# L1 attention: TensorE's small products in a new order over the two images of a pair

## The chip, the cores and the metric

The kernel runs on one core of one Trainium2 chip. The metric is the device time of one execution in microseconds (us). The kernel before takes 2540.39 us, the median of 3 runs (2538.69 to 2540.77).

## What is computed

Two layers of a small vision tower over 128 images of 64 tokens with 64 features: wavelet tokens, linear attention and a mixture of experts (layer 0), then attention by L1 distances and a routed network (layer 1). The change touches the L1 attention alone:

```python
v = (x @ wqv_w.T + wqv_b).reshape(b, t, 3 * h, d)
q, vf, vb = (v[:, :, :h], v[:, :, h:2 * h], v[:, :, 2 * h:])
k = x[:, :, None, :] * wk[None, None]
a = _l1_scores(q, k)              # a[s, t, h] = -sum_w |q[s, h, w] - k[t, h, w]| / sqrt(64)
a = jnp.concatenate([a, jnp.zeros((b, 1, t, h), a.dtype)], axis=1)
a = jax.nn.softmax(a, axis=1)[:, :t]
bf = jnp.einsum('bsdh,bshw->bdhw', a, vf)
bb = jnp.einsum('bdsh,bshw->bdhw', a, vb)
o = (bf + bb).sum(axis=2).reshape(b, t, d)
y = o * jax.nn.sigmoid(1.702 * o)
y = y @ fanin_w.T + fanin_b
return x + y                      # here x is the normalised h, and the result is added to h
```

With 8 heads, one image has 64 x 64 x 8 distances over 64 features: 2,097,152 absolute differences.

## The kernel before, in words

The stage works on pairs of images, 64 in all. Pair q is done image by image (b = 0, 1), and an image in 16 steps k = 0 to 15, whose kinds stand in `ORDER = "DADDADDADDADADED"`. In every step TensorE multiplies `blocks` (queries and keys of the image, each as a high and a low fp16 part, spread by DMA) by a matrix of ones and minus ones (`pick`), so that 1024 columns of differences come out in two PSUM banks. There are three kinds of step:

- D (ten in an image, called D0 to D9 here, at k = 0, 2, 3, 5, 6, 8, 9, 11, 13, 15; L850): VectorE takes absolute values and sums in one reduction (`reduce`, L1548). There are two pairs of banks (0 and 1, 2 and 3), so D number i waits until reduction i-2 has ended (`red`).
- A (A0 to A4, at k = 1, 4, 7, 10, 12; L838): ScalarE writes the absolute values of banks 4 and 5 to `absd` (`absolute`, L1133), and GpSimd adds them up in a tree (`batch`, L1665, L1669), once for an image, when all five are there. Each half of an A waits for ScalarE's operation on the same bank before it (`abs`).
- E (k = 14, L842): as A, with the features on the partitions; ScalarE writes `abse` (L1136). The sums over these are made by TensorE: `sum_e` (L810) into bank 7, `copy_e` on ScalarE (L1143), `turn_e` (L817), `take_e` on ScalarE into `score` (L1151, semaphore `etaken`).

Between these steps TensorE makes small products, one pair ahead or some pairs behind. They are called from `extra(b, k)`, right behind step k of image b. For pair q+1: `turn` (transposes x, bank 7; ScalarE copies it in `prepare_x`), `queries` (L735; ScalarE `high_q`), `low` for the queries (L744; subtracts the high part in PSUM, ScalarE copies the rest, L1112), `keys` (L739; `high_k`), `low` for the keys. These share bank 6, so each waits for ScalarE's copy of the one before (`half`). For pair q-1: the values, `values_b` (L751, copy to `vb` L1118) and `values_f` (L758, copy to `vf` L1122), also in bank 6, and `sum_e`, `turn_e`. For pair q-2: `turn_attn` (L766) and `attend` in three parts (L784, L789) with the normalised exponentials of GpSimd (`normalise`); ScalarE's `gate_o` and VectorE's `gated` follow. For pair q-3: `turn_y` (L795), `turned_y` on ScalarE, `fan_in` (L799) and `finish` on VectorE (L1543, semaphore `sum`), which adds the result to h. ScalarE also does the exponentials of pair q-1 in four parts (L1163).

Every engine works through its own list in the order in which it is written, and a wait holds all that stands behind it. The orders are written out by hand: on TensorE in `extra`, on ScalarE and VectorE in their `pair`. SP issues the spreading of queries and keys (`fill_blocks`, 8 DMAs for an image) and of the scores (`spread`, 4 for a pair). Pairs 4 to 63 run in a loop of two pairs a turn, the first four are written out, and behind the loop the last pairs' small products are finished ahead of the routed network.

Of the kernel before, what the change touches and what calls it, by code (L numbers as in the profile page):

```python
# [121 lines left out]
def build(nc, a, out, scratch):  # L122

    with ExitStack() as ctx:
# [376 lines left out]
        def _(pe):  # L501
# [220 lines left out]
            def turn(p, at):  # L722

                if at >= 3:
                    pe.wait_ge(X["sum"], p - 3)
                if at == 2:
                    pe.wait_ge(X["etaken"], p - 2)
                pe.wait_ge(X["xs"], 16 * (p + 1))
                pe.transpose(ps[7][:, 0:P], xs1[:], ident[:]).then_inc(X["xT_ps"], 1)
# [16 lines left out]
            def values_b(p, odd, at):  # L746

                pe.wait_ge(X["half"], 4 * (p + 2))
                if at >= 3:
                    pe.wait_ge(X["attq"], p - 1)  # L750
# [18 lines left out]
            def attend(p, odd, part):  # L769


                if part == 0:
                    pe.wait_ge(X["etaken"], p + 2)
                    pe.wait_ge(X["attq"], p + 1)
                    pe.wait_ge(X["xTq"], 2 * p + 8)
# [25 lines left out]
            def sum_e(p, first):  # L801

# [3 lines left out]
                if not first:  # L806
                    pe.wait_ge(X["etaken"], p)
# [47 lines left out]
            def pair(q, odd, at):  # L855
                def extra(b, k):
                    if b == 0:
                        if k == 0 and at >= 1:
                            values_b(q - 1, 1 - odd, at)
                        if k == 1 and at >= 3:  # L860
                            turn_y(q - 3)
                        if k == 4 and at >= 3:
                            fan_in(q - 3)
                        if k == 5 and at >= 1:
                            values_f(q - 1, 1 - odd)
                        if k == 8:
                            turn(q + 1, at)
                        if k == 10:
                            queries(q + 1, at)
                        if k == 11 and at >= 1:  # L870
                            sum_e(q - 1, at == 1)
                        if k == 13 and at >= 1:
                            turn_e(q - 1)
                        if k == 12:
# [3 lines left out]
                    else:  # L878
                        if k == 0:
                            low(q + 1, 1 - odd, 1)  # L880
                        if at >= 2:
                            if k == 5:
                                turn_attn(q - 2)
                            if 7 <= k < 10:
                                attend(q - 2, odd, k - 7)

# [14 lines left out]
            values_b(last, 1, 4)  # L901
            turn_y(last - 2)
            values_f(last, 1)
            fan_in(last - 2)
            pe.wait_ge(X["sum"], last - 1)
            sum_e(last, False)
# [77 lines left out]
        def _(act):  # L984
# [196 lines left out]
            def pair(q, odd, at):  # L1181
                s, first = 2 * q, at == 0
                absolute(s, 0, 0, q, first)
                if at >= 1:
                    values_b(q - 1, 1 - odd, at < 3)
                if at >= 3:
                    turned_y(q - 3)
                absolute(s, 0, 1, q, first)
                if at >= 1:
                    values_f(q - 1, 1 - odd)  # L1190
                absolute(s, 0, 2, q, first)
                prepare_x(q + 1, 1 - odd)
                absolute(s, 0, 3, q, first)
                high_q(q + 1, False)
                if at >= 1:
                    copy_e(q - 1)
                absolute(s, 0, 4, q, first)
                low(q + 1, 0)
                if at >= 1:
                    take_e(q - 1, 1 - odd, at - 1)  # L1200
                absolute(s, 0, 5, q, first)
                s += 1
                high_k(q + 1)
                low(q + 1, 1)
                absolute(s, 1, 0, q, first)
                absolute(s, 1, 1, q, first)
                if at >= 2:
                    turned_attn(q - 2)
                absolute(s, 1, 2, q, first)
                if at >= 1:  # L1210
                    exponentials(q - 1, 0, at == 1)
# [3 lines left out]
                if at >= 1:  # L1215
                    exponentials(q - 1, 1, at == 1)
                absolute(s, 1, 4, q, first)
                if at >= 1:
                    exponentials(q - 1, 2, at == 1)
                absolute(s, 1, 5, q, first)  # L1220
                if at >= 1:
                    exponentials(q - 1, 3, at == 1)

# [12 lines left out]
            values_b(last, 1, False)  # L1236
            turned_y(last - 2)
            values_f(last, 1)
# [47 lines left out]
        def _(dve):  # L1286
# [265 lines left out]
            def pair(q, odd, slot, at):  # L1552
                for b in range(2):
# [3 lines left out]
                    for d in range(ND):  # L1557
                        reduce(2 * q + b, odd, b, d)
                        if b == 0 and d == 0 and at >= 2:
                            reciprocals(q - 2)  # L1560
                        if b == 0 and d == 3 and at >= 3:
# [174 lines left out]
```

## Time and profile before

| what | value |
|---|---|
| median of 3 runs | 2540.39 us (2538.69 to 2540.77) |
| the profiled execution | 2541.08 us, of which the span is 2539.3 us |
| TensorE busy (matmul), in the span | 2232.0 us (88%) |
| VectorE busy | 2096.2 us (83%) |
| ScalarE busy | 1634.4 us (64%) |
| GpSimd busy | 1765.2 us (70%) |
| mean granted TensorE clock | 0.967 |
| first and last reduction of the stage (L1548) | 720.3 us, 2431.5 us |

The profile is of one execution. A row of its timeline has the start, the duration, the engine and the line of the kernel, the operation, what it writes and reads, how many like instructions were merged (x2), and in brackets the idle time of the engine ahead of it with what ended it. Matmuls are pipelined: the end of a row of TensorE reaches under the next one's start, so the time that an instruction costs is read from start to start. Two matmuls that belong together (a D, an A) are one row of x2.

### The profile page before, as it was taken

What the parts mean: (1) busy time and instruction counts of PE and PEld (TensorE: products, weight loads), DVE (VectorE), ACT (ScalarE), POOL (GpSimd) and SP (SyncE); (2) the same over time, 40 slices, a digit from 0 to 9 for tenths busy, and PEclk for the clock granted to TensorE, in tenths of its full rate; (3) what the DMA queues carried; (4) which work ended last, traced back from release to release, by engine and by line L of the source; (5) the groups of instructions that cost most, each with busy time, mean ns of one, the idle gap of its engine ahead of it and who ended that gap; (6) DMA issues with size and microseconds to landing.
All of it is one profiled execution on the core that took longest, in us unless ns stands there. A gap on an engine that the chain in (4) does not pass through costs nothing.

```text
span 2539.3 us, 48447 instructions
## 1 busy us (share of the span) xinstructions
PE 2232.0 (88%) x13527; PEld 999.4 (39%) x13527; DVE 2096.2 (83%) x2515; ACT 1634.4 (64%) x4156; POOL 1765.2 (70%) x1033
## 2 busy tenths in 40 slices
PE   5567999999468999999999999999999999999978
PEld 3443333333123344433343344434333444343347
DVE  2887777777878888888888888888888888888874
ACT  0324555555247777777777777777777777777756
POOL 0111333333358998998989989989899899899853
PEclk8788999999779999999999999999999999999989
DMA  4300000000011221122112211221221122112201
GB/s 126 74 1 1 1 0 0 0 0 0 0 45 49 54 53 48 49 52 52 48 49 53 52 47 50 53 50 48 50 53 50 47 52 53 48 48 52 53 18 32
DMA packets 151074, 102.04 MB, mean 40 GB/s; under 512 B 43629, under 2 KB 149038, under 8 KB 150895
## 3 DMA queue, kind: packets, MB, share of 16 engines
q1 hardware_dynamic: 150714, 101.37, 16.0%
q8 instruction: 22, 0.36, 0.1%
q10 hardware_dynamic: 316, 0.12, 0.0%
q14 instruction: 22, 0.18, 0.0%
HBM read 10.64 MB, written 4.19 MB: 6 GB/s over the span
## 4 chain that ended last, share of the span: by engine, by line
PE 52%; DVE 24%; issue 12%; ACT 9%; DMA 1%; DVEq 1%; ACTq 0%; POOL 0%; SPq 0%; POOLq 0%
DVE score L1548 19%; PE pp L850 10%; ACT absd L1133 6%; PE pp L658 5%; PE pp L838 4%; PE pp L789 3%; PE pp L739 3%; PE pp L810 3%; PE pp L679 3%; PE pp L683 2%; PE pp L735 2%; PE pp L684 2%; PE pp L680 2%; PE pp L650 2%; PE pp L784 2%
## 5 line engine op out<-in xcount | busy, mean ns | idle before, releaser
L1548 DVE TENSOR_REDUCE score<-pp 128x16 f32<-128x1024 f32 x1280 | 1498.8, 1217 | 214.2 <-PE pp L850 212.8
L1665 POOL TENSOR_TENSOR absd<-absd 128x2560 f32<-128x2560 f32 x635 | 1442.8, 2272 | 162.1 <-ACT absd L1133 122.1
L1133 ACT ACTIVATE absd<-pp 128x512 f32<-128x512 f32 x1280 | 696.0, 598 | 274.2 <-PE pp L838 274.1
L850 PE MATMUL pp<-blocks,pick 128*128 128x512 f16 x2560 | 750.5, 382 | 100.8 <-DVE score L1548 82.1
L838 PE MATMUL pp<-blocks,pick 128*128 128x512 f16 x1280 | 394.8, 382 | 9.3 <-ACT absd L1133 0.5
L850 PEld LDWEIGHTS pp<-blocks,pick 128*128 128x128 f16 x2560 | 196.7, 98 | 467.3 <-DVE score L1548 312.9
L1632 POOL TENSOR_TENSOR absd<-absd,yw 128x512 f32<-128x512 f32 x112 | 142.4, 1271 | 319.0 <-DVE yw L1470 319.0
L1064 ACT ACTIVATE absd<-pp 128x512 f32<-128x512 f32 x256 | 150.8, 596 | 148.1 <-PE pp L680 145.7
L1486 DVE SCALAR_TENSOR_TENSOR absd<-pp,absd 128x512 f32<-128x512 f32 x256 | 172.4, 687 | 53.3 <-ACT absd L1064 38.4
L838 PEld LDWEIGHTS pp<-blocks,pick 128*128 128x128 f16 x1280 | 114.7, 97 | 207.1 <-ACT absd L1133 59.8
L1163 ACT ACTIVATE expd<-attn 128x65 f32<-128x65 f32 x512 | 162.9, 337 | 0.0
L1136 ACT ACTIVATE absd<-pp 128x512 f32<-128x512 f32 x256 | 143.9, 638 | 0.0
L658 PE MATMUL pp<-absd 128*64 128x512 f32 x512 | 138.1, 618 | 0.0
L842 PE MATMUL pp<-pick,blocks 128*128 128x256 f16 x512 | 88.6, 274 | 29.8 <-ACT absd L1133 23.7
L1163 ACT ACTIVATION_READ_ACCUMULATOR expd<-attn 128x1 f32 x512 | 111.5, 218 | 0.0
L679 PE MATMUL pp<-x,absd 128*128 128x512 f16 x256 | 98.4, 384 | 0.6
L1112 ACT CAST qk<-pp 128x512 f16<-128x512 f32 x130 | 77.3, 595 | 32.4 <-PE pp L744 32.4
L683 PE MATMUL pp<-x,absd 128*128 128x512 f16 x256 | 97.8, 382 | 0.3
L684 PE MATMUL pp<-x,absd 128*128 128x512 f16 x256 | 97.5, 381 | 0.0
L680 PE MATMUL pp<-x,absd 128*128 128x512 f16 x256 | 97.5, 381 | 0.0
L1068 ACT COPY absd<-pp 128x512 f32<-128x512 f32 x128 | 75.0, 586 | 28.0 <-PE pp L650 19.1
L1470 DVE TENSOR_TENSOR yw<-pp,absd 128x512 f32<-128x512 f32 x112 | 77.1, 689 | 17.6 <-PE pp L658 15.2
(234 smaller groups left out, 2721.9 us busy)
## 6 DMA issues: line engine op xcount, KB each, us to landing
blocks<-qk SPq DMA_DIRECT2D x1032, 64.0 KB, 2.0
attn<-score SPq DMA_DIRECT2D x256, 64.0 KB, 2.2
xs<-xn SPq DMA_DIRECT2D x66, 32.0 KB, 1.8
big<-in_wrb_t SPq DMA_DIRECT2D x1, 2064.0 KB
big<-in_x_rows SPq DMA_DIRECT2D x4, 512.0 KB, 6.1
token_rows<-big SPq DMA_DIRECT2D x8, 256.0 KB, 2.0
big<-in_L_ffn_w SPq DMA_DIRECT2D x4, 512.0 KB, 10.2
out<-h SPq DMA_DIRECT2D x16, 128.0 KB, 2.0
```

The lines of the kernel that those rows point to most:

```text
L658: mm = pe.matmul(ps[4 + k % 2][64 * e:64 * e + 64, :], w3[:, 2 * k + e, :], hid[:, 2 * (k % 2) + e, :], start=True, stop=True)
L679: pe.matmul(ps[e], w12_hi[:, 0, 2 * k + e, :], x2[:, b, :], start=True, stop=False)
L680: pe.matmul(ps[e], w12_lo[:, 0, 2 * k + e, :], x2[:, b, :], start=False, stop=True).then_inc(C["h1_ps"], 1)
L683: pe.matmul(ps[2 + e], w12_hi[:, 1, 2 * k + e, :], x2[:, b, :], start=True, stop=False)
L838: mm = pe.matmul(ps[4 + n], pick[:, unit % 8, :], blocks[:, b, unit // 16, unit // 8 % 2, :], start=True, stop=True)
L850: mm = pe.matmul(ps[bank + n], pick[:, unit % 8 + n, :], blocks[:, b, unit // 16, unit // 8 % 2, :], start=True, stop=True)
L1064: nc.scalar.activation(silu[:, e, :], ps[e], ACT.Silu, scale=1.0 / W_SCALE).then_inc(C["silu"], 1)
L1133: nc.scalar.activation(absd[odd][:, 16 * u + 8 * n:16 * u + 8 * n + 8, :], ps[4 + n].rearrange("p (h w) -> p h w", w=D), ACT.Abs).then_inc ...
L1163: op = nc.scalar.activation(expd[:, n, :], attn[:, :, n], ACT.Exp, scale=-(float(D) ** -0.5), accum_out=zst[:, 0, n:n + 1])
L1486: dve.scalar_tensor_tensor(out=hid[:, 2 * (k % 2) + e, :], in0=ps[2 + e], scalar=1.0 / W_SCALE, in1=silu[:, e, :], op0=ALU.mult, op1=ALU.m ...
L1548: dve.tensor_reduce(score[:, odd, b, 16 * d:16 * d + 16], pp[:, bank:bank + 2, :].rearrange("p n (h w) -> p (n h) w", w=D), AX.X, ALU.add, ...
L1665: nc.gpsimd.tensor_tensor(x[:, :, 0:w], x[:, :, 0:w], x[:, :, w:2 * w], ALU.add).then_inc(X["tree"], 1)
```

## The change

On TensorE, the values of pair q are made at the end of pair q itself, in image 1 (`values_b` behind k = 11, `values_f` behind k = 14), no longer in image 0 of pair q+1. `sum_e` and `turn_e` move from k = 11 and 13 of image 0 to k = 5 and 7, ahead of `turn`, which moves from 8 to 9; `queries` moves from 10 to 11, the first `low` from 12 to 13, the second from k = 0 of image 1 to k = 1, `turn_attn` from 5 to 4. `turn_y` comes at the end of image 1 and `fan_in` at k = 1. The waits follow: `turn` waits for the last `etaken`; `sum_e` waits from the fourth pair on for `sum` at p - 1; `attend` loses two waits. ScalarE's and VectorE's lists are put in the same order: the copies of the values and of y go to image 1, the exponentials move up by a step, with one part behind the copy of vb and ahead of A4; the reciprocals come behind D1, `finish` behind D2. No instruction of the stage is added or removed.

```diff
@@ TensorE
             def turn(p, at):
-                if at >= 3:
-                    pe.wait_ge(X["sum"], p - 3)
-                if at == 2:
-                    pe.wait_ge(X["etaken"], p - 2)
+                if at >= 1:
+                    pe.wait_ge(X["etaken"], p - 1)
...
             def values_b(p, odd, at):
                 pe.wait_ge(X["half"], 4 * (p + 2))
-                if at >= 3:
+                if at >= 2:
                     pe.wait_ge(X["attq"], p - 1)
...
                 if part == 0:
-                    pe.wait_ge(X["etaken"], p + 2)
                     pe.wait_ge(X["attq"], p + 1)
-                    pe.wait_ge(X["xTq"], 2 * p + 8)
...
-            def sum_e(p, first):
+            def sum_e(p, at):
                 pe.wait_ge(X["abs"], 4 * NA * (p + 1))
-                if not first:
-                    pe.wait_ge(X["etaken"], p)
+                if at >= 3:
+                    pe.wait_ge(X["sum"], p - 1)
...
                     if b == 0:
-                        if k == 0 and at >= 1:
-                            values_b(q - 1, 1 - odd, at)
                         if k == 1 and at >= 3:
-                            turn_y(q - 3)
-                        if k == 4 and at >= 3:
                             fan_in(q - 3)
                         if k == 5 and at >= 1:
-                            values_f(q - 1, 1 - odd)
-                        if k == 8:
+                            sum_e(q - 1, at)
+                        if k == 7 and at >= 1:
+                            turn_e(q - 1)
+                        if k == 9:
                             turn(q + 1, at)
-                        if k == 10:
+                        if k == 11:
                             queries(q + 1, at)
-                        if k == 11 and at >= 1:
-                            sum_e(q - 1, at == 1)
-                        if k == 13 and at >= 1:
-                            turn_e(q - 1)
-                        if k == 12:
+                        if k == 13:
                             low(q + 1, 1 - odd, 0)
                         if k == 14:
                             keys(q + 1, 1 - odd)
                     else:
-                        if k == 0:
+                        if k == 1:
                             low(q + 1, 1 - odd, 1)
                         if at >= 2:
-                            if k == 5:
+                            if k == 4:
                                 turn_attn(q - 2)
                             if 7 <= k < 10:
                                 attend(q - 2, odd, k - 7)
+                        if k == 11:
+                            values_b(q, odd, at)
+                        if k == 14:
+                            values_f(q, odd)
+                        if k == 15 and at >= 2:
+                            turn_y(q - 2)
...
             last = PAIRS - 1
-            values_b(last, 1, 4)
-            turn_y(last - 2)
-            values_f(last, 1)
             fan_in(last - 2)
-            pe.wait_ge(X["sum"], last - 1)
-            sum_e(last, False)
+            sum_e(last, 4)
@@ ScalarE
                 absolute(s, 0, 0, q, first)
-                if at >= 1:
-                    values_b(q - 1, 1 - odd, at < 3)
-                if at >= 3:
-                    turned_y(q - 3)
                 absolute(s, 0, 1, q, first)
                 if at >= 1:
-                    values_f(q - 1, 1 - odd)
+                    copy_e(q - 1)
                 absolute(s, 0, 2, q, first)
+                if at >= 1:
+                    take_e(q - 1, 1 - odd, at - 1)
                 prepare_x(q + 1, 1 - odd)
                 absolute(s, 0, 3, q, first)
                 high_q(q + 1, False)
-                if at >= 1:
-                    copy_e(q - 1)
                 absolute(s, 0, 4, q, first)
                 low(q + 1, 0)
-                if at >= 1:
-                    take_e(q - 1, 1 - odd, at - 1)
                 absolute(s, 0, 5, q, first)
+                high_k(q + 1)
                 s += 1
-                high_k(q + 1)
+                absolute(s, 1, 0, q, first)
                 low(q + 1, 1)
-                absolute(s, 1, 0, q, first)
                 absolute(s, 1, 1, q, first)
                 if at >= 2:
                     turned_attn(q - 2)
+                if at >= 1:
+                    exponentials(q - 1, 0, at == 1)
                 absolute(s, 1, 2, q, first)
                 if at >= 1:
-                    exponentials(q - 1, 0, at == 1)
+                    exponentials(q - 1, 1, at == 1)
                 absolute(s, 1, 3, q, first)
                 if at >= 2:
                     gate_o(q - 2)
-                if at >= 1:
-                    exponentials(q - 1, 1, at == 1)
-                absolute(s, 1, 4, q, first)
+                values_b(q, odd, at < 2)
                 if at >= 1:
                     exponentials(q - 1, 2, at == 1)
+                absolute(s, 1, 4, q, first)
                 absolute(s, 1, 5, q, first)
+                values_f(q, odd)
                 if at >= 1:
                     exponentials(q - 1, 3, at == 1)
+                if at >= 2:
+                    turned_y(q - 2)
...
@@ VectorE
                         reduce(2 * q + b, odd, b, d)
-                        if b == 0 and d == 0 and at >= 2:
+                        if b == 0 and d == 1 and at >= 2:
                             reciprocals(q - 2)
-                        if b == 0 and d == 3 and at >= 3:
+                        if b == 0 and d == 2 and at >= 3:
                             finish(q - 3, slot)
```

## Rows read from the trace of the kernel before

**Rows 1.** Busy time, clock by stretch; columns as in its first line.

```profile
core 0: us, PE busy (x) PEld busy (x) DVE busy (x) ACT busy (x) POOL busy (x), PEclk, DMA share, GB/s
800.00:1600.00 800.00, 736.41 (x4786) 319.92 (x4784) 705.59 (x687) 591.77 (x1609) 725.98 (x390) 1.00 0.20 50
...
2440.00:2539.00 99.00, 78.17 (x563) 65.52 (x558) 49.31 (x86) 60.42 (x188) 35.67 (x50) 0.87 0.10 23
```

**Rows 2.** Timeline of VectorE (DVE): start, us, engine, line, operation, operands, [idle before <-releaser].

```profile
826.13 0.19 DVE L1533 RECIPROCAL zst<-zst 128x8 f32<-128x8 f32 x1
...
1335.31 3.44 DVE L1548 TENSOR_REDUCE score<-pp 128x16 f32<-128x1024 f32 x3
1338.66 0.21 DVE L1543 TENSOR_TENSOR h<-pp,h 128x64 f32 x1
...
1344.64 1.22 DVE L1548 TENSOR_REDUCE score<-pp 128x16 f32<-128x1024 f32 x1 [0.98 <-PE pp L850]
1347.01 9.28 DVE L1548 TENSOR_REDUCE score<-pp 128x16 f32<-128x1024 f32 x8 [1.14 <-PE pp L850]
1356.64 1.23 DVE L1548 TENSOR_REDUCE score<-pp 128x16 f32<-128x1024 f32 x1 [0.36 <-PE pp L850]
...
1359.68 2.36 DVE L1548 TENSOR_REDUCE score<-pp 128x16 f32<-128x1024 f32 x2 [0.46 <-PE pp L850]
...
2380.14 0.19 DVE L1533 RECIPROCAL zst<-zst 128x8 f32<-128x8 f32 x1
```

**Rows 3.** Timeline of TensorE (PE), image 0 of a pair.

```profile
1337.09 1.08 PE L758 MATMUL pp<-wqv,xT 96*64 96x256 f32 x8
...
1340.94 1.02 PE L735 MATMUL pp<-wqv,xTq 96*128 96x512 f32 x2
1341.80 0.60 PE L850 MATMUL pp<-blocks,pick 128*128 128x512 f16 x2
1342.33 1.09 PE L810 MATMUL pp<-absd,pair_ones 128*32 128x256 f32 x16
...
1344.01 0.59 PE L850 MATMUL pp<-blocks,pick 128*128 128x512 f16 x2
1344.44 0.51 PE L817 MATMUL pp<-row_of,esum 128*128 128x16 f32 x4
1344.81 0.60 PE L842 MATMUL pp<-pick,blocks 128*128 128x256 f16 x4
1345.41 1.13 PE L739 MATMUL pp<-wk_diag,xT 96*128 96x512 f32 x2
1346.37 1.03 PE L850 MATMUL pp<-blocks,pick 128*128 128x512 f16 x4
```

**Rows 4.** Timeline of TensorE, D7 to D9 of image 1.

```profile
1356.01 0.59 PE L850 MATMUL pp<-blocks,pick 128*128 128x512 f16 x2
...
1357.36 0.59 PE L850 MATMUL pp<-blocks,pick 128*128 128x512 f16 x2
1358.33 0.88 PE L842 MATMUL pp<-pick,blocks 128*128 128x256 f16 x4 [0.38 <-ACT absd L1133]
1359.05 1.11 PE L850 MATMUL pp<-blocks,pick 128*128 128x512 f16 x4
```

**Rows 5.** Timeline of ScalarE (ACT), the same pair.

```profile
1338.22 0.59 ACT L1122 COPY vf<-pp 128x512 f32<-128x512 f32 x1 [0.93 <-PE pp L758]
...
1342.14 0.60 ACT L1104 ACTIVATE qk<-pp 128x512 f16<-128x512 f32 x1
...
1357.07 0.33 ACT L1163 ACTIVATE expd<-attn 128x65 f32<-128x65 f32 x1
...
1357.67 1.09 ACT L1133 ACTIVATE absd<-pp 128x512 f32<-128x512 f32 x2
```

**Rows 6.** Timeline of GpSimd (POOL); the idle time comes once a pair.

```profile
1332.09 11.68 POOL L1665 TENSOR_TENSOR absd<-absd 128x2560 f32<-128x2560 f32 x5 [1.55 <-ACT absd L1133]
```

**Rows 7.** Timeline of VectorE behind the last pair.

```profile
2434.73 0.23 DVE L1543 TENSOR_TENSOR h<-pp,h 128x64 f32<-128x64 f32 x1 [1.78 <-PE pp L799]
```

**Rows 8.** Timeline of SP's queue: the spreading of one image's queries and keys.

```profile
1347.08 5.34 SPq L452 DMA_DIRECT2D blocks<-qk  x8
```

More of the change, by code:

```diff
@@ L1235, in _ @@
             last = PAIRS - 1
-            values_b(last, 1, False)
-            turned_y(last - 2)
-            values_f(last, 1)
             copy_e(last)
```

## The prediction

> **What bounds the kernel now.** I read first the windows by stage, then the timeline of VectorE over one pair, then TensorE's and ScalarE's beside it, then GpSimd's. L1 attention fills about 1720 us of the 2539.3 us span, in 64 like pairs; the reader is to see in [rows 1] that in its middle the clock is 1.00 and no engine is full. The period is read from VectorE: between the reciprocals at 826.13 and those at 2380.14 lie 58 pairs [rows 2], so one takes 26.79 us. VectorE is busy for 705.6 of 800 us [rows 1], which is 23.6 of them. The other 3.1 are a few waits that are alike in every pair, the largest of them 0.98 and 1.14 at D8 and D9 of image 0, and 0.36 and 0.46 at D7 and D9 of image 1 [rows 2]. (D0 to D9 are the ten products of an image that VectorE reduces, A0 to A4 those that ScalarE takes, E its last.) Each of these waits ends with a product of TensorE. GpSimd has 1.55 us idle a pair [rows 6]; it isn't the bound, but a floor at about 25.25.
>
> **Why the stalls are where they are.** VectorE has two pairs of banks: D(i) may start when reduction i-2 has ended. A reduction takes 1.23, the next starts 1.15 to 1.16 after it (eight in 9.28), a matmul that waits starts 0.06 after it, and a reduction starts 0.63 after its D starts (1344.01 to 1344.64, 1346.37 to 1347.01) [rows 2, 3]. So a D that starts as soon as it may, 1.29 after the start of reduction i-2, is ready 1.92 after it and wanted 2.30 after it: TensorE's credit is never more than 0.38 us. Over n D's in a row it may spend 1.15 n + 0.38 from one D to another; what is beyond is a stall that nothing later gives back. This is the rule by which I cost the change. It accounts for the rows: from D8 to D9 of image 0 there are 2.36 us [rows 3], VectorE was already waiting at D8, so 2.36 - 1.15 = 1.21 of stall, and 1.14 is there.
>
> Durations, from a start to the next start: a D or an A 0.43 (0.53 ahead of an fp32 product); values_b and queries 0.86 (a row of 1.02 of which 0.16 lies under the next, as in the 1.13 of keys, which take 0.96 to the next start); values_f and sum_e 1.02 (rows of 1.08 and 1.09, of which 0.07 lie under the next); turn_e 0.37 [rows 3]; a 128x512 operation of ScalarE 0.59, the next 0.49 after it starts (two in 1.09); two exponentials 0.60; from the start of a large fp32 product to ScalarE's copy of it 1.13 to 1.20 (1337.09 to 1338.22, 1340.94 to 1342.14), I take 1.18 [rows 3, 5]; from the start of an A to its absolute values 0.42.
>
> **Image 1, after the change.** Up to D7 the order is as before but that low moves behind A0 and turn_attn one slot forward, both within the credit (0.43 + 0.22 + 0.43 from D0 to D1; 0.43 + 0.69 + 0.43 from D2 to D3, where D1 to D2 take 0.43); D7 starts 9.00 after the start of D9's reduction of image 0, as now (1347.01 to 1356.01), and stalls 0.36 as now [rows 2, 4]. Now come the moved values, which are 1.88 us of TensorE:
> - D7 0.53, values_b 0.86, A4 0.43, then D8: 1.82 from D7 to D8 where there are 1.35 now [rows 4]. D8 is reduced at 11.46; gated lies between and gives 0.2, so the stall is 0.48.
> - ScalarE does A3, gate_o, **the copy of vb, two exponentials, and only then A4**. The copy can start at 9.53 + 1.18 = 10.71, leaves ScalarE free at 11.20, the exponentials at 11.80. The absolute values of A4 then start at 11.80, although A4 itself was there at 10.8. They end at 12.40 and 12.89. E overwrites their banks, so it waits: its halves go at 12.46 and 12.95, until 13.17. TensorE stands 1.2 us. (Now E waits 0.38, [rows 4].)
> - values_f then stands ahead of D9: 13.17 + 1.02 = 14.19. The reduction of D9 starts at 14.82, and was due at 11.46 + 1.15 = 12.61: stall 2.2.
> So image 1 takes 14.82 where it takes 12.67 (1347.01 to 1359.68) [rows 2]: **+2.15**.
>
> **Image 0, after the change**, zero at the start of D9's reduction of image 1. turn_y (0.28) and fan_in (0.27) lie in the time that D1 waits for its bank; yT is ready at 1.0, when fan_in comes. No cost. D3 may start at 3.59. Then **sum_e**, which now has a wait for finish of the pair three before. Finish stands behind D2's reduction, which starts at 3.56 (the reciprocals, 0.11, are before it): it ends at 3.56 + 1.14 + 0.21 = 4.91 and sum_e starts at 4.97, 0.85 after TensorE was ready. Behind it are queued D4 and all else. D4 at 5.99, reduced at 6.62 and due at 5.99: stall 0.63. A2 and turn_e (0.43 + 0.53 + 0.37) delay D5 by another 0.17; turn, A3 and D6, D7 then keep up. Queries start at 9.76, A4 at 10.62, D8 at 11.05, reduced at 11.68: 0.29 late, for the 1.82 between D7 and D8 (2.21 now, [rows 3]). **low** must wait for high_q: 9.76 + 1.18 + 0.60 + 0.06 = 11.60, just in time. ScalarE does A4 after high_q, at 11.41 to 12.38, and only then low's copy, to 12.98. Keys wait for it (E's halves, at 12.07 and 12.56, are through at 12.78): 13.04, D9 at 14.00, reduced at 14.63, due at 12.83: stall 1.8. Sum_e and turn_e, which gave this chain its cover, have left it. Image 0 takes 14.63 where it takes 14.08 to 14.20: **+0.5**. The 1.88 us of values that left it don't come back as time, because they stood at D0 and D3, where the credit covers them: with them D0 to D2 take 1.8 + 0.43 and D3 to D5 1.55 + 0.87, and 2.68 are allowed.
>
> Sum: 14.82 + 14.63 = 29.45 us a pair against 26.79, **+2.65**. The other way, stalls of 0.36 + 0.48 + 2.2 + 0.63 + 0.17 + 0.29 + 1.8 = 5.9 on 23.6 give 29.5.
>
> **What is moved without cost.** SP's queue keeps its order; its last spreads wait for etaken, which comes earlier, and the blocks of the next image 0 wait for low's copy, about 1 us later in image 1, with a whole image (over 14 us) until they are needed, 5.3 of issue [rows 8] and 2 to land. If that cover were gone every pair would pay it; nothing in the order suggests that. GpSimd's floor of 25.25 is far below 29.4. Its trees start later with A4 and end well ahead of the next normalise's use. The waits for etaken and xTq that attend loses were long past.
>
> **Ends of the stage.** 63 pairs at 2.65 are 167; pair 0 has the new values but no exponentials and no attend, by the same steps about +2. Behind the last pair, values_b and values_f no longer stand ahead of fan_in, for which VectorE waited 1.78 [rows 7]: -2. The profiled execution took 2541.08 (span 2539.3 and 1.8 around it), so 2541.1 + 167 = 2708; it lies 0.7 above the median of the runs, so **2707**.
>
> **Bounds.** The latency to ScalarE (1.13 to 1.20) enters three chains: +-0.1 a pair. That ScalarE would take A4 with its operation already decoded or not: +-0.1. Whether turn_y costs 0.11 (as in the gap behind its row) or 0.28: nothing at one end, 0.17 at the other. That the wait of sum_e isn't hit: -0.7. A further wait of that size between two queues: +0.7. So the period is 28.6 to 30.3, the case's own range 2653 to 2760.
>
> **Rivals.**
> - *Faster: the loads are what counts.* TensorE has now some 13.0 us of work in image 0 and 9.8 in image 1 (32 times 0.217 for D, A and E, and the small products beside them); afterwards 11.0 and 11.8, and VectorE needs 11.8 for either. If the ring had the credit to even this out within an image, all stalls would go and GpSimd would bound: 1.55 a pair over 60 pairs [rows 6], 2541 - 93 = 2448. For it: neither load is above VectorE's. Against it: the 0.38 of credit, by which the present stalls come out to 0.1. It decides if D8 to D9 takes less than 1.53 in both images. The Trainium skill ("Perfetto Trace Analysis", Identifying the Most-Contended Engine) would have the time follow the engine with the highest occupancy, which here is this case; the present trace, with no engine above 0.92 in the stage, doesn't bear that out.
> - *Milder.* The two waits between engines don't bite (E behind the exponentials, 1.2; sum_e behind finish, 0.7): 27.5 a pair, 2541 + 45 = 2586. For it: they are my reading of two queues, not a row. A time within 0.2% of before would need these and a little more.
> - *Much slower: the clock.* With TensorE waiting over 1 us twice a pair, the granted clock could fall below 1.00. It was 0.87 behind 2440 us, where TensorE is busy 0.79 of the time [rows 1]. At 0.87 its 22.8 us a pair would be 3.4 more, a part of it in waits: 2780 to 2920. Against it: busy for 24.7 of 29.4 us it would still be at 0.84.
>
> **Chances.** The forecast 0.75; milder 0.09 (of which same 0.02); faster 0.10; clock 0.05; the remaining 0.01 with same. The range must leave out no more than 0.2: the forecast's own range and the upper half of the milder case, 2610 to 2760. What a measurement can tell from no change is about 0.2%. Faster 0.10, same 0.03, slower 0.87.
>
> **What the profile after would show.** A period near 29.4. In image 1 the ScalarE rows vb, exponentials, absolute values in this order, and about 1.2 us of TensorE idle ahead of E, released by ScalarE; a VectorE wait of 2.2 ahead of D9. In image 0 TensorE idle 0.85 ahead of sum_e, released by finish, a VectorE wait of 0.6 at D4 and 1.8 at D9. GpSimd idle 4.2 a pair. Wrong if the waits ahead of D9 are below 0.4 in both images, or if the rows show another engine's wait that makes up the period.

## The result, and the profile after

The kernel after takes 2686.84 us (median, 2686.23 to 2687.28) against 2540.12 us of the kernel before beside it: 1.0579 times, 95% interval 1.0562 to 1.0596. It is slower by 147 us, in the range of the forecast and 20 us below its number. The profiled execution's span is 2684.7 us, 145.4 more than before.

Busy time and clock in the middle of the stage and behind it, with the columns of [rows 1]:

```profile
800.00:1600.00 800.00, 690.17 (x4379) 293.06 (x4377) 650.98 (x633) 547.82 (x1479) 669.01 (x358) 1.00 0.19 46
...
2585.00:2684.00 99.00, 80.10 (x590) 66.98 (x588) 51.07 (x86) 60.88 (x189) 35.47 (x50) 0.85 0.10 24
```

Every engine is less busy than in [rows 1], by much the same factor: 0.92 for VectorE and GpSimd, 0.93 for ScalarE, 0.94 for TensorE. Nothing was added; all have got more time to wait. The granted clock is 1.00 here too, so the difference doesn't come from the clock.

VectorE over one pair of the kernel after (L1518, L1523, L1528 and L1533 are reciprocals, gated, finish and reduce), the lines that answer to [rows 2]:

```profile
1340.23 9.28 DVE L1533 TENSOR_REDUCE score<-pp 128x16 f32<-128x1024 f32 x8 [1.75 <-PE pp L844]
1349.86 1.23 DVE L1533 TENSOR_REDUCE score<-pp 128x16 f32<-128x1024 f32 x1 [0.36 <-PE pp L844]
1351.00 0.21 DVE L1523 SCALAR_TENSOR_TENSOR osb<-osb,pp 128x64 f32<-128x64 f32 x1
1351.59 1.23 DVE L1533 TENSOR_REDUCE score<-pp 128x16 f32<-128x1024 f32 x1 [0.37 <-PE pp L844]
1354.92 3.49 DVE L1533 TENSOR_REDUCE score<-pp 128x16 f32<-128x1024 f32 x3 [2.11 <-PE pp L844]
1358.33 0.19 DVE L1518 RECIPROCAL zst<-zst 128x8 f32<-128x8 f32 x1
1358.44 1.17 DVE L1533 TENSOR_REDUCE score<-pp 128x16 f32<-128x1024 f32 x1
1359.53 0.21 DVE L1528 TENSOR_TENSOR h<-pp,h 128x64 f32 x1
1359.66 1.21 DVE L1533 TENSOR_REDUCE score<-pp 128x16 f32<-128x1024 f32 x1
1361.56 4.71 DVE L1533 TENSOR_REDUCE score<-pp 128x16 f32<-128x1024 f32 x4 [0.69 <-PE pp L844]
1366.43 1.22 DVE L1533 TENSOR_REDUCE score<-pp 128x16 f32<-128x1024 f32 x1 [0.16 <-PE pp L844]
1369.41 9.28 DVE L1533 TENSOR_REDUCE score<-pp 128x16 f32<-128x1024 f32 x8 [1.76 <-PE pp L844]
```

From 1340.23 to 1369.41 is the period, 29.18 us. Image 1 is the stretch from its start to 1354.92, 14.69 us, and ends with the waits 0.36, 0.37 and 2.11 ahead of D7, D8 and D9; image 0 is the rest, 14.49 us, with 0.69 ahead of D4, 0.16 ahead of D8 and 1.76 ahead of D9.

TensorE in the same pair, first D7 to D9 of image 1 (answering to [rows 4]), then sum_e of image 0 (to [rows 3]):

```profile
1349.23 0.60 PE L844 MATMUL pp<-blocks,pick 128*128 128x512 f16 x2
1349.66 1.02 PE L749 MATMUL pp<-wqv,xT 96*128 96x512 f32 x2
1350.52 0.60 PE L832 MATMUL pp<-blocks,pick 128*128 128x512 f16 x2
1350.96 0.59 PE L844 MATMUL pp<-blocks,pick 128*128 128x512 f16 x2
1352.46 0.88 PE L836 MATMUL pp<-pick,blocks 128*128 128x256 f16 x4 [0.91 <-ACT absd L1123]
1353.27 1.08 PE L756 MATMUL pp<-wqv,xT 96*64 96x256 f32 x8
1354.28 0.60 PE L844 MATMUL pp<-blocks,pick 128*128 128x512 f16 x2
...
1358.47 0.60 PE L844 MATMUL pp<-blocks,pick 128*128 128x512 f16 x2
1359.88 1.09 PE L804 MATMUL pp<-absd,pair_ones 128*32 128x256 f32 x16 [0.81 <-DVE h L1528]
```

And ScalarE between A3 and E of image 1 (answering to [rows 5]):

```profile
1350.72 0.58 ACT L1108 COPY vb<-pp 128x512 f32<-128x512 f32 x1 [0.31 <-PE pp L749]
1351.20 0.33 ACT L1153 ACTIVATE expd<-attn 128x65 f32<-128x65 f32 x1
...
1351.82 1.07 ACT L1123 ACTIVATE absd<-pp 128x512 f32<-128x512 f32 x2
```

A4 (1350.52) could have been taken from 1350.94 on; it is taken at 1351.82, behind the copy of vb and two exponentials. E waits 0.91 for it, values_f (1353.27) stands behind E, and D9 (1354.28) behind that: 3.32 us from D8 to D9, where [rows 4] have 1.69. In image 0, sum_e waits 0.81 for finish (1359.53, done at 1359.74).

GpSimd's idle time, 1.55 in [rows 6], is now two gaps in a pair:

```profile
1338.18 11.71 POOL L1650 TENSOR_TENSOR absd<-absd 128x2560 f32<-128x2560 f32 x5 [1.34 <-ACT absd L1123]
...
1352.97 10.22 POOL L1650 TENSOR_TENSOR absd<-absd 128x2560 f32<-128x2560 f32 x3 [2.60 <-ACT absd L1123]
```

### The profile page after: what moved, and what is told of

Its sections match the earlier page's. It is cut to its first block, busy times and chain, and to the rows that moved or that the text cites. A ratio compares the mean times of both kernels' runs of the same rounds, so it can differ in the third digit from the quotient of the medians.

```text
span 2684.7 us, 48355 instructions
## 1 busy us (share of the span) xinstructions
PE 2261.5 (84%) x13527; PEld 997.1 (37%) x13527; DVE 2100.7 (78%) x2515; ACT 1645.1 (61%) x4156; POOL 1766.6 (66%) x1033
## 4 chain that ended last, share of the span: by engine, by line
PE 56%; DVE 22%; issue 12%; ACT 8%; DMA 1%; DVEq 1%; ACTq 0%; POOL 0%; SPq 0%; POOLq 0%
DVE score L1533 17%; PE pp L844 11%; PE pp L658 5%; ACT absd L1123 4%; PE pp L832 3%; PE pp L784 3%; PE pp L737 3%; PE pp L804 2%; PE pp L679 2%; PE pp L756 2%; PE pp L683 2%; PE pp L733 2%; PE pp L749 2%; PE pp L680 2%; PE pp L684 2%
## 5 line engine op out<-in xcount | busy, mean ns | idle before, releaser
L1533 DVE TENSOR_REDUCE score<-pp 128x16 f32<-128x1024 f32 x1280 | 1503.9, 1217 | 359.2 <-PE pp L844 357.8
L836 PE MATMUL pp<-pick,blocks 128*128 128x256 f16 x512 | 100.4, 278 | 76.0 <-ACT absd L1123 57.4
L804 PE MATMUL pp<-absd,pair_ones 128*32 128x256 f32 x1024 | 70.0, 383 | 50.0 <-DVE h L1528 50.0
L1153 ACT ACTIVATION_READ_ACCUMULATOR expd<-attn 128x1 f32 x512 | 102.2, 200 | 0.0
L1133 ACT COPY esum<-pp 128x256 f32<-128x256 f32 x64 | 23.8, 372 | 114.3 <-PE pp L804 114.3
```

Of the source, the lines that this page charges most:

```text
L1153: op = nc.scalar.activation(expd[:, n, :], attn[:, :, n], ACT.Exp, scale=-(float(D) ** -0.5), accum_out=zst[:, 0, n:n + 1])
L1533: dve.tensor_reduce(score[:, odd, b, 16 * d:16 * d + 16], pp[:, bank:bank + 2, :].rearrange("p n (h w) -> p (n h) w", w=D), AX.X, ALU.add, ...
```

## The experiments

Theory: VectorE's two pairs of banks let TensorE fall behind by 0.38 us (the credit) before VectorE waits, and the period grows by what stands in a row beyond it; of the places where it does, one hangs on ScalarE's order, one on finish, and the rest on where the values and the other small products stand. First rival: what counts is how much work TensorE has in an image. Second rival: the waits overlap, so that taking one away only makes the next longer.

**Exponentials behind A4.** The kernel after, on ScalarE:

```diff
                 values_b(q, odd, at < 2)
-                if at >= 1:
-                    exponentials(q - 1, 2, at == 1)
                 absolute(s, 1, 4, q, first)
+                if at >= 1:
+                    exponentials(q - 1, 2, at == 1)
```

> The kernel after, with one edit on ScalarE: the two exponentials that stand between the copy of vb and the absolute values of A4 in image 1 are put behind A4. Theory (order of the queues): A4's absolute values start 0.62 us earlier, so E, values_f and D9 do too, and VectorE's wait ahead of D9 of image 1 falls from 2.11 to 1.5 us. Period 29.18 to 28.56, 2687 to about 2649 us. Rival (what counts is how much work TensorE has in image 1, not ScalarE's order): TensorE's list is unchanged, so the time stays at 2687 within 5 us.

Measured: 2648.86 us. VectorE's line ahead of D9 of image 1 in this kernel:

```profile
1343.29 3.49 DVE L1533 TENSOR_REDUCE score<-pp 128x16 f32<-128x1024 f32 x3 [1.52 <-PE pp L844]
```

2.11 has become 1.52, TensorE's wait ahead of E has fallen from 0.91 to 0.31, and 38 us have gone. TensorE's list is unchanged to the last instruction, so the first rival can't account for it.

**A4 ahead of the values too.** The kernel after, on ScalarE:

```diff
-                values_b(q, odd, at < 2)
-                if at >= 1:
-                    exponentials(q - 1, 2, at == 1)
                 absolute(s, 1, 4, q, first)
+                values_b(q, odd, at < 2)
+                if at >= 1:
+                    exponentials(q - 1, 2, at == 1)
```

> The kernel after, with one edit on ScalarE: A4's absolute values come ahead of both the copy of vb and the exponentials. Theory: E hardly waits for ScalarE's work on values any more (its idle time of 0.91 us falls to about 0.2), but values_f now waits for the copy of vb: from 1351.9 on ScalarE, so D9 starts about 0.7 us earlier, not 1.2. Wait ahead of D9 2.11 to 1.4, period 28.5, time about 2643 us. Rival (amount of work): 2687. If E's wait were all of it: 2687 - 62 * 1.2 = 2613.

Measured: 2645.39 us. TensorE, E and values_f of image 1:

```profile
1337.04 0.88 PE L836 MATMUL pp<-pick,blocks 128*128 128x256 f16 x4
1338.00 1.08 PE L756 MATMUL pp<-wqv,xT 96*64 96x256 f32 x8
```

E no longer waits as long, but values_f starts 0.96 after E instead of 0.81: it waits for the copy of vb, which ScalarE now starts at 1337.36 and ends 0.05 ahead of it. So only 0.7 of the 0.91 comes back, as expected: the place of A4 on ScalarE is worth 41 us of the 147, and the wait ahead of D9 is still 1.40. That this rest is due to values_f's own place is argued from the two rows, not tested by itself.

**Finish one step earlier.** The kernel after, on VectorE:

```diff
-                        if b == 0 and d == 1 and at >= 2:
+                        if b == 0 and d == 0 and at >= 2:
                             reciprocals(q - 2)
-                        if b == 0 and d == 2 and at >= 3:
+                        if b == 0 and d == 1 and at >= 3:
                             finish(q - 3, slot)
```

> The kernel after, with one edit on VectorE: reciprocals behind D0 and finish behind D1 (now behind D1 and D2), so that sum_e on TensorE finds its semaphore set. Theory: TensorE's 0.81 us of idle ahead of sum_e and VectorE's wait of 0.69 at D4 go; D5 to D9 of image 0 are paced from D4, so all of it comes through: period 29.18 to 28.5, about 2644 us. Rival (the later wait at D9, 1.75 us, swallows it, since keys wait for ScalarE anyway): the wait ahead of D9 grows by what D4 loses, and the time stays at 2687 within 8 us.

Measured: 2637.41 us, 49 less than the kernel after, and 7 better than expected. VectorE's image 0:

```profile
1341.86 0.21 DVE L1528 TENSOR_TENSOR h<-pp,h 128x64 f32 x1
1341.99 6.92 DVE L1533 TENSOR_REDUCE score<-pp 128x16 f32<-128x1024 f32 x6
1349.07 1.22 DVE L1533 TENSOR_REDUCE score<-pp 128x16 f32<-128x1024 f32 x1 [0.17 <-PE pp L844]
1352.05 9.28 DVE L1533 TENSOR_REDUCE score<-pp 128x16 f32<-128x1024 f32 x8 [1.76 <-PE pp L844]
```

D2 to D7 run as one row of six. The wait ahead of D9 is 1.76 as before: it did not swallow the 0.69, and the second rival falls for image 0. The image takes 13.67 us (1338.38 to 1352.05) instead of 14.49, 0.82 less. That is 0.13 more than the 0.69 in brackets. Of this 0.08 is the end of a reduction: ahead of a wait its whole 1.23 us counts, in a run it takes 1.15 to the next start. So a wait costs its bracket and 0.08. The other 0.05 lies in gaps too short for a bracket.

**Both at once.** The last two edits together.

> The kernel after with both edits at once: on ScalarE A4's absolute values ahead of the copy of vb and the exponentials, on VectorE reciprocals behind D0 and finish behind D1. Theory (the waits stand in different images and add up, since VectorE is caught up between them): 2687 - 42 - 50 = 2595 us, period about 27.7, still above the 26.79 of the kernel before, because values_b and values_f still stand where TensorE has no room (waits at D8 and D9 of image 1 of 0.4 and 1.4) and queries, low and keys lie without cover in image 0. Rival (they overlap): not below 2630.

Measured: 2593.83 us. The two alone took 41.5 and 49.4 us, together 93.0: they add up. What stays, 1.0216 times the kernel before (interval 1.0195 to 1.0236), is left to the order of the products itself. VectorE ahead of D9 of image 1:

```profile
1351.46 2.35 DVE L1533 TENSOR_REDUCE score<-pp 128x16 f32<-128x1024 f32 x2 [1.41 <-PE pp L844]
```

Beside it stay 0.37 at D8 of image 1 and 1.76 at D9 of image 0, the latter where queries, low and keys follow on each other. No run undoes that order in the kernel after alone.

**The values alone.** The kernel before, with only values_b and values_f and their copies at the end of their own pair, and with ScalarE's list of image 1, the exponentials too, as in the kernel after:

```diff
@@ TensorE
                     if b == 0:
-                        if k == 0 and at >= 1:
-                            values_b(q - 1, 1 - odd, at)
...
-                        if k == 5 and at >= 1:
-                            values_f(q - 1, 1 - odd)
...
                     else:
+                        if k == 11:
+                            values_b(q, odd, at)
+                        if k == 14:
+                            values_f(q, odd)
@@ ScalarE, image 1: as in the kernel after from absolute(s, 1, 1) to exponentials(q - 1, 3)
```

> The kernel before, with the values alone moved: values_b behind k = 11 and values_f behind k = 14 of image 1 of their own pair, with ScalarE's order of image 1 as in the kernel after; sum_e, turn_e, turn, queries, low, keys, turn_attn, turn_y and finish as before. Theory (credit of 0.38 us): image 1 grows by 2.0 us (waits 0.37 at D8, 2.1 at D9) and image 0 gains next to nothing from the 1.9 us that left it, as its waits at D7 to D9 come from queries, sum_e and keys. Period 26.79 to 28.8, about 2665 us. Rival (load): image 0 loses 1.9 of its 13 us on TensorE, so its waits of 2.3 us go for the most part, and the time stays within 40 us of 2540 or falls.

Measured: 2665.53 us. VectorE (reduce is L1542 here):

```profile
1344.21 1.23 DVE L1542 TENSOR_REDUCE score<-pp 128x16 f32<-128x1024 f32 x1 [0.38 <-PE pp L850]
1347.55 2.36 DVE L1542 TENSOR_REDUCE score<-pp 128x16 f32<-128x1024 f32 x2 [2.11 <-PE pp L850]
...
1357.05 1.23 DVE L1542 TENSOR_REDUCE score<-pp 128x16 f32<-128x1024 f32 x1 [0.16 <-PE pp L850]
1359.26 1.22 DVE L1542 TENSOR_REDUCE score<-pp 128x16 f32<-128x1024 f32 x1 [0.98 <-PE pp L850]
1361.69 1.23 DVE L1542 TENSOR_REDUCE score<-pp 128x16 f32<-128x1024 f32 x1 [1.21 <-PE pp L850]
```

Image 1 has the waits of the kernel after to 0.01, and image 0, from which 1.9 us of TensorE's work have gone, has kept its waits: 0.16 and 0.98, and 1.21 where [rows 2] have 1.14. This is the verdict on the first rival: taking work out of an image doesn't help where it isn't taken out of the run that overspends. The values, with the order of ScalarE that goes with them, make 126 of the 147 us; the rest of the change makes the other 21.

**The credit itself, measured by added work.** To the kernel before, in every pair, four products that nobody reads:

```diff
+            def extra_work():
+                for n in range(4):
+                    pe.matmul(ps[7][:, 384:512], ident[:], ident[:], start=True, stop=True)
```

called in one kernel behind k = 2 of image 1 (`d_early`), in the other behind queries in image 0 (`d_late`).

> The kernel before, with extra work added that nothing reads: four fp32 products of 128 columns (identity by identity, into columns 384 to 511 of bank 7) behind k = 2 of image 1, in every pair. By the row of turn_attn (0.43 to 0.69) and of queries (0.86 for 512 columns) they take 0.4 to 0.9 us of TensorE. Theory (credit): they stand where D0 to D3 leave room, 1.08 + 0.43 + extra up to 1.0 is below 2.68, so they cost nothing: 2540 within 5 us. Rival (TensorE's total work sets the period): 0.4 to 0.9 us a pair, 2567 to 2600 us.

> The same added work, but behind queries (k = 10) of image 0, where D6 to D9 already take more than the credit. Theory: all of it becomes a wait of VectorE, 0.4 to 0.9 us a pair, 2567 to 2600 us (less what low no longer waits for ScalarE). Rival (total work): the same time as for the other place. A rival by which small products are hidden wherever they stand: 2540.

Measured: 2538.48 us at the first place (0.9994 times before, interval 0.9984 to 1.0005), 2597.73 us at the second. TensorE at the first place, then at the second:

```profile
1347.12 1.05 PE L858 MATMUL pp<-ident 128*128 128x128 f32 x8
...
1334.11 1.05 PE L858 MATMUL pp<-ident 128*128 128x128 f32 x8
1335.00 0.59 PE L850 MATMUL pp<-blocks,pick 128*128 128x512 f16 x2
```

VectorE ahead of D7 of image 0 in the kernel before, then in the kernel with the products at the second place:

```profile
1342.44 1.23 DVE L1548 TENSOR_REDUCE score<-pp 128x16 f32<-128x1024 f32 x1 [0.16 <-PE pp L850]
...
1335.64 1.23 DVE L1554 TENSOR_REDUCE score<-pp 128x16 f32<-128x1024 f32 x1 [1.05 <-PE pp L850]
```

The products take 0.89 us to the next start at either place (1334.11 to 1335.00; at the first place D2 starts at 1348.01). Early in image 1 they cost nothing; among queries, sum_e and keys VectorE's wait grows from 0.16 to 1.05, all of the 0.89, and 58 us in all. The same work, 0 or 58 us.

**Keys where there is room.** The kernel before:

```diff
@@ TensorE
-                        if k == 14:
-                            keys(q + 1, 1 - odd)
                     else:
                         if k == 0:
+                            keys(q + 1, 1 - odd)
+                        if k == 3:
                             low(q + 1, 1 - odd, 1)
@@ ScalarE
+                absolute(s, 1, 0, q, first)
                 high_k(q + 1)
                 low(q + 1, 1)
-                absolute(s, 1, 0, q, first)
```

> The kernel before, with keys moved from k = 14 of image 0 to k = 0 of image 1 and the second low from k = 0 to k = 3 of image 1, ScalarE's copies with them. Theory: D8 to D9 of image 0 fall from 2.36 to 1.4 us, and D9, D0 of image 1 with 0.44 + 1.92 lie within 2.68: the wait ahead of D9 falls from 1.14 to about 0.25, with 0.06 at D1. Period 26.79 to about 25.95, 2488 us. Rival (each pair's queries and keys then reach their blocks too late, as SP's queue issues them up to 2.5 us later): a wait of TensorE for the DMA at the start of image 0, and no gain.

Measured: 2494.64 us, 0.9818 times the kernel before (interval 0.9801 to 0.9834); 7 us short of what was expected. VectorE:

```profile
1353.24 8.28 DVE L1548 TENSOR_REDUCE score<-pp 128x16 f32<-128x1024 f32 x7 [0.98 <-PE pp L850]
1361.86 1.22 DVE L1548 TENSOR_REDUCE score<-pp 128x16 f32<-128x1024 f32 x1 [0.33 <-PE pp L850]
```

The wait ahead of D9 of image 0 is gone wholly (D8, D9 and D0 to D4 of image 1 are one row of seven), but one of 0.33 is new at D5 of image 1: low now waits for high_k, A1, the copy of the turned attention and the first part of attend come later. TensorE waits for the DMA of `blocks` once in the whole run, for 3.3 us, as it does in the kernel before: no such wait has come up in the pairs.

**And the exponentials out of the way of A4.** As the last, and on ScalarE exponentials part 1 ahead of A3:

```diff
+                if at >= 1:
+                    exponentials(q - 1, 1, at == 1)
                 absolute(s, 1, 3, q, first)
                 if at >= 2:
                     gate_o(q - 2)
-                if at >= 1:
-                    exponentials(q - 1, 1, at == 1)
                 absolute(s, 1, 4, q, first)
```

> As the kernel with keys in image 1, and on ScalarE the second part of the exponentials moved from behind A3 to ahead of A3, into ScalarE's idle time of 1.77 us. Theory: A4's absolute values start when A3's are through, E's wait of 0.38 shrinks, D9 of image 1 is in time (its wait of 0.46 goes). With keys: period about 25.5, 2460 us, still above GpSimd's floor of 25.25 (2444 us). Rival: GpSimd becomes the bound earlier, since it starts its tree when A4 is there: 2475 or more.

Measured: 2478.91 us, 0.9758 times the kernel before (interval 0.9741 to 0.9774). The period is 25.85 us, not 25.5: the wait of 0.46 is gone, the new 0.33 at D5 is there, and another of 0.16 behind the reciprocals. By its number the rival would fit (2475 or more), but GpSimd still waits for ScalarE in every pair, so it isn't the bound:

```profile
1336.78 11.66 POOL L1665 TENSOR_TENSOR absd<-absd 128x2560 f32<-128x2560 f32 x5 [0.48 <-ACT absd L1133]
```

**Half of sum_e moved: a miss.** To the last kernel. Turn now writes columns 384 to 511 of bank 7, so that it may stand between the halves, and the first half waits for finish (`sum`), as in the kernel after:

```diff
+                        if k == 6 and at >= 1:
+                            sum_e(q - 1, at == 1, 0, at >= 3)
                         if k == 11 and at >= 1:
-                            sum_e(q - 1, at == 1)
+                            sum_e(q - 1, at == 1, 1, at >= 3)
@@ sum_e
-                for m in range(4):
+                for m in range(2 * half, 2 * half + 2):
@@ VectorE
-                        if b == 0 and d == 3 and at >= 3:
+                        if b == 0 and d == 2 and at >= 3:
                             finish(q - 3, slot)
```

> As the kernel with keys in image 1 and the exponentials ahead of A3, and half of sum_e (two of its four groups of products) moved from k = 11 to k = 6 of image 0, where D3 to D5 have about 0.5 us of room; finish goes behind D2, x is transposed into other columns of bank 7. Theory: the wait of 0.98 at D8 falls to about 0.47, period 25.85 to 25.35, 2448 us. There GpSimd comes in as the bound (its work is about 25.3 a pair). Rival (sum_e waits for finish as in the kernel after, or the half is dearer than 0.51): 2465 or more.

Measured: 2525.41 us, 46 more than without the split. TensorE:

```profile
1332.15 1.06 PE L813 MATMUL pp<-absd,pair_ones 128*32 128x256 f32 x8
1333.15 0.61 PE L842 MATMUL pp<-blocks,pick 128*128 128x512 f16 x2
...
1336.57 1.06 PE L813 MATMUL pp<-absd,pair_ones 128*32 128x256 f32 x8
1337.56 0.60 PE L842 MATMUL pp<-blocks,pick 128*128 128x512 f16 x2
```

Half of the products (x8 of x16) take 1.00 and 0.99 us, the whole takes 1.02. The halves didn't wait for finish: there is no bracket. Work was doubled, not shared out. VectorE waits 0.74 at D5 and 0.95 at D8.

**The same, with attend one step later.** To the kernel of the split:

```diff
-                            if 7 <= k < 10:
-                                attend(q - 2, odd, k - 7)
+                            if 8 <= k < 11:
+                                attend(q - 2, odd, k - 8)
@@ ScalarE
-                if at >= 2:
-                    gate_o(q - 2)
                 absolute(s, 1, 4, q, first)
+                if at >= 2:
+                    gate_o(q - 2)
@@ VectorE
-                        if b == 1 and d == 7 and at >= 2:
+                        if b == 1 and d == 8 and at >= 2:
                             gated(q - 2)
```

> As the kernel before it in this list, and attend one step later (k = 8, 9, 10), gate_o behind A4, gated behind D8: attend no longer waits for the copy of the turned attention, and VectorE's wait of 0.33 at D5 of image 1 goes. Theory: VectorE's waits alone would give 25.0 a pair, but GpSimd's work of 25.3 now bounds: 2440 to 2450 us, hardly below the one before; GpSimd's idle time ahead of its trees falls to almost nothing. Rival (GpSimd isn't a bound): 2427.

Measured: 2509.73 us. The expected time was built on that of the split and missed with it. Against the last kernel it gains 16 us: the waits of 0.34 at D5 and 0.36 at D7 of image 1 become one of 0.76 at D8. The one of 0.16 behind the reciprocals goes as well. Moving work within a run that overspends leaves the run's excess.

**Cut by columns.** The kernel of the split, with the halves cut the other way:

```diff
-                for m in range(2 * half, 2 * half + 2):
+                at = slice(P * half, P * half + P)
+                for m in range(4):
                     for b in range(2):
-                        mm = pe.matmul(ps[7][32 * m:32 * m + 32, 0:2 * P], pair_ones[:, b, :], abse[b][:, m, :],
+                        mm = pe.matmul(ps[7][32 * m:32 * m + 32, at], pair_ones[:, b, :], abse[b][:, m, at],
```

> As the kernel that split sum_e, but the halves are cut by columns (all four groups of 32 partitions, 128 of 256 columns) and not by groups. In the kernel cut by groups each half took 0.99 us from start to next start (1332.15 to 1333.15, 1336.57 to 1337.56), the whole in one piece 1.02. Theory (the four groups run beside each other on TensorE, and the columns set the time): a half by columns takes about 0.55, VectorE's wait of 0.74 at D5 of image 0 falls to 0.3 or less and the one of 0.95 at D8 to about 0.5, period 26.35 to about 25.5, 2525 to about 2460 us, below the 2479 of the kernel without a split. Rival (each half has a fixed cost of its own of some 0.9, whatever its size): 2525.

Measured: 2474.35 us, 0.9743 times the kernel before (interval 0.9727 to 0.9759), the fastest of all.

```profile
1340.44 0.66 PE L814 MATMUL pp<-absd,pair_ones 128*32 128x128 f32 x16
1341.03 0.60 PE L843 MATMUL pp<-blocks,pick 128*128 128x512 f16 x2
...
1344.44 0.66 PE L814 MATMUL pp<-absd,pair_ones 128*32 128x128 f32 x16
1345.04 0.61 PE L843 MATMUL pp<-blocks,pick 128*128 128x512 f16 x2
```

A half takes 0.60 us from start to next start. VectorE from D5 of image 0 on:

```profile
1342.11 3.67 DVE L1556 TENSOR_REDUCE score<-pp 128x16 f32<-128x1024 f32 x3 [0.34 <-PE pp L855]
```

The waits are 0.34 at D5 and 0.55 at D8, together 0.25 less than the 0.16 and 0.98 without a split. Yet the kernel beats the one without a split by 4.6 us only, 0.07 a pair, and not by 19. (The intervals of the two ratios overlap; from the first reciprocals to the last the traces have 1611.9 us against 1616.1.) The line shows the missing 0.18: three reductions in a row take 3.49, D5 to D7 take 3.67 here, in gaps too short for a bracket. On TensorE, A3 and queries take 1.47 (1342.45 to 1343.92) where they take 1.29 without the split (1345.56 to 1346.85); why, no run shows.

## Why the prediction was right, point by point

**The credit rule** carried it. Its sum was 29.45 us a pair; the trace has 29.18. Nearly all the places that it named have their wait, and the largest are at the size forecast: 2.11 for 2.2, 1.76 for 1.8, 0.69 for 0.63, 0.37 for 0.48, 0.36 for 0.36. One forecast wait isn't there (0.17 at D5), one is smaller (0.16 for 0.29 at D8). That the total came so near owes something to errors of 0.1 that went both ways, as the next two points show.

**Image 1** takes 14.69, not 14.82. Two terms were too large. D7 was put at 0.53 ahead of values_b, as ahead of an fp32 product; it takes 0.43 (1349.23 to 1349.66). That "0.53 ahead of an fp32 product" was read from rows ahead of values_f and sum_e, and doesn't hold for values_b and queries. It is also why D8 waits 0.37 and not 0.48. The second is the latency from values_b to its copy: 1349.66 to 1350.72 is 1.06, where I took 1.18 from the rows of values_f and queries. Whether ScalarE is idle ahead of the copy doesn't explain it: queries at 1335.33 have theirs 1.20 later, though ScalarE waited for it:

```profile
1336.53 0.60 ACT L1094 ACTIVATE qk<-pp 128x512 f16<-128x512 f32 x1 [0.66 <-PE pp L733]
```

The latency differs by product, 1.06 to 1.20, and why stays open. One term was too small: E to values_f takes 0.81, not 0.71. The rest of the chain, copy, exponentials, A4, E, values_f, D9, is as told; the first two experiments confirm it by moving its links.

**Image 0** takes 14.49, not 14.63: queries start (1364.50) 9.58 behind the start of D9's reduction and not at 9.76, since the wait at D5 isn't there; behind queries the chain is as long as forecast (4.91 for 4.87). That sum_e would wait for finish (0.85 forecast, 0.81 measured) was read from two queues, not from a row, and is shown by the experiment on finish. Its worth was put at 0.7 a pair; measured it is 0.8, as the exposed end of a reduction comes on top. The same 0.08 is why the rule gave 1.21 for the kernel before where the bracket says 1.14.

**That the values which left image 0 would give nothing back** is shown by the run that moves them alone: image 0 keeps its waits.

**The ends.** I counted 63 pairs at 2.65, +2 at the start and -2 at the end. In the traces, up to the first reciprocals of the stage the kernel after loses 4.2 us (52.4 to 56.6 from the first reduction), between them and the last but one 145.7 (61 pairs at 2.37, and 1.2 for a shorter one at the end), behind that it gains 3.5, and the stage starts 1.0 earlier, which I can't assign to the change. So some 17 us of the error are 0.28 a pair over 61 pairs, and most of the rest comes from counting 63 full pairs.

**The rivals.** Load: falls with the run of the values alone, and with the two places of the added products. The clock: it was granted at 1.00 in the stage, with waits of 0.91 and 0.81 on TensorE in every pair. The milder case: both waits between engines are there, and the experiments on ScalarE's order and on finish price them at 41 and 49 us.

GpSimd was said to be idle 4.2 us a pair; it is 1.34 + 2.60 and two gaps of some 0.16.

What stays open: why the latencies and the time of queries differ as told, why the stage starts 1.0 us earlier, and whether with the rest of the waits gone GpSimd would bound at 25.25, which no run reached (25.8 was the shortest period).

## What to carry to other kernels

With two buffers between a producer and a consumer, and neither engine busy all the time, the time isn't set by either engine's sum but by runs: note the work between each two hand-overs, and any run that spends more than the consumer's time plus the small credit (here 0.38 us) is paid in full, while room elsewhere is lost (the same products cost 0 or 58 us here). So small jobs go singly where the producer waits anyway, not in a row at the end. Where an in-order engine gets a new item, look at what stands behind it (here A4 behind a copy and two exponentials), and at who waits for that.

## What the runs showed of the hardware

The four groups of sum_e write to different 32 partitions of PSUM, and by their times they run beside each other: all four take 1.02 us, two of them 1.00 and 0.99, all four with half the columns 0.60. Work that is packed so gets shorter when cut by columns, and not when cut by groups. The Trainium skill says this for such products ("TensorE: Matmul & The Clock Gate", Packing small matmuls), that tiles of the array at different positions run concurrently; the traces agree. The expectation for the split had taken half the instructions for half the time.

The same 0.89 us of fp32 products cost 0 or 58 us by place, and a wait of VectorE costs 0.08 us more than its bracket, since in a run of reductions (1.15 from start to start) the end of each (1.23 long) lies under the next.
